# One core, a Mamba-2 block beside a gated feed-forward layer: the order of the first batch is rewritten, and one product moves to GpSimd

## The chip, the core and the metric

The kernel runs on one core of a Trainium2 chip. Its time is device time in microseconds (us). A core has four compute engines that run their own instruction streams side by side and meet through semaphores: TensorE (matrix products into the eight PSUM banks of 512 fp32 columns), VectorE, ScalarE and GpSimd; SyncE's queue and ScalarE's queue start the transfers. In the profile they are PE (and PEld for weight loads), DVE, ACT, POOL and SP.

## The reference

`x` has 4 sequences of 512 tokens with 512 channels. Everything is fp32.

```python
xn  = (x - mean(x)) / sqrt(var(x) + 1e-5)                  # over the 512 channels
out = x + (xn + mamba2(xn)) + ffn(xn)

def mamba2(u):                                             # 16 heads of 64, state 128
    z, xBC, dt = split(u @ w_in)                           # 1024, 1024 + 128 + 128, 16
    dt  = softplus(dt + dt_bias)
    xBC = silu(causal_conv4(xBC, conv_w) + conv_b)         # 4 taps along the tokens
    X, B, C = split(xBC)
    y = ssd(X * dt, dt * -exp(A_log), B, C) + X * D        # state-space scan
    y = y * silu(z)
    y = y * rsqrt(mean(y * y) + 1e-5) * norm_w
    return y @ w_out

def ffn(u):
    h = silu(u @ W1.T) * (u @ W3.T)                        # 2048 wide
    return fwht(h) @ W2.T                                  # Walsh-Hadamard over 2048
```

## The kernel before, in words

The four sequences ("batches") run one after the other. Each matrix product is made in three fp16 passes: the operands are split into a high and a low half (`hi`, `lo`), and hi*hi, hi*lo and lo*hi are summed in PSUM (`three`, L541). So that the halves fit fp16, each weight group is scaled by a power of two that comes from a bound on its sum of squares. This costs the first batch much preparation which the others don't have: it reads the fp32 weights, squares and sums them, scales and splits them, and writes the halves to `w_parts` in HBM, from which batches 1 to 3 load them.

The unit of work is a weight tile: 128 output channels by 512 tokens, 12 matmuls of 512 columns. Ten C tiles (x, B, C, with the convolution), eight Z tiles (the gate), sixteen pairs A, U (W1, W3), then sixteen G steps (W2). All engines walk one list per batch, `SCHEDULES[b]`, and each executes its own part of each token; that list alone sets the order on each engine. In batch 0 it begins with `FIRST`; behind it, tokens are placed by the count of A and U and G tiles before them (`FIRST_AT`, `STEP_AT`, `PREP_AT`). The tokens the change touches:

- `C`, `Z`, `A`, `U`: TensorE projects a tile (`project`); ScalarE and VectorE finish it (`finish`). For C, ScalarE starts an accumulator (L860), VectorE adds three taps (L1121), ScalarE makes a tanh (L875) and VectorE the silu (L1103), which frees one of two accumulators. In batch 0 ScalarE and VectorE first split the tile that is `AHEAD` = 3 places further on (L823, L1084).
- `G1S`: ScalarE squares the last two pieces of the second w_in group, TensorE sums them (L580), VectorE makes the second scale (`scale_g1`), which all tiles from the fifth on need for their split. The first scale, of four tiles and w_dt, is made before the loop.
- `KA`, `K`, `KS`: squares of W1 (ScalarE, L897) and W3 (GpSimd, L1294) from a ring of five buffers, their sums on TensorE (L636, L641), and the scale of W1 and W3.
- `DT`, `SUM`: projection of dt, softplus, cumulative sums. `WOL`, `WOQ`, `WOS`, `WOH`: load, squares, scale and split of w_out.
- `F`: half of the Hadamard transform of one W2 block: TensorE multiplies (L649), ScalarE squares the block for the W2 scale (L800) and copies the product (L908) into one of two buffers, SyncE stores it to `w2_mid` (L503). `H`: the other half (L661, L917, L1185). `W2S` makes the W2 scale that H needs.
- `T`, `X`, `S`, `R`, `Y`, `N`, `Q`, `V`, `W`: the scan, four chunks of 128 tokens per batch. `T` includes XD = X * D on ScalarE (L951) and Xdec on GpSimd (L1309); TensorE needs Xdec at `S`, VectorE XD at `Y`.
- `LN`, `XT`: normalisation of the next sequence (VectorE L998 to L1009, ScalarE L757) and its transposes (TensorE L555), copied out as `xh` (ScalarE L763) and `xl` (VectorE L1015).

A tile's PSUM bank is one of three in turn, so TensorE waits at a tile for the eviction of the tile, or F product, three places before (`make_banks`, `claim`). H has bank 4 alone.

## Time and profile before

| | us |
|---|---|
| median of 3 runs | 1010.45 (1009.56 to 1012.27) |
| the profiled execution | 1006.74 |
| its span | 1004.9 |

| engine | busy, us | share |
|---|---|---|
| PE | 941.8 | 94% |
| DVE | 597.8 | 59% |
| ACT | 391.2 | 39% |
| POOL | 264.3 | 26% |

The span runs from the first to the last instruction. A busy TensorE says only that matmuls were under way; a matmul at the lower of its two clocks (1.2 instead of 2.4 GHz) is busy twice as long. The granted clock is shown as a share of 2.4 GHz. An idle time is put down to the instruction that ended it, the releaser. Rows beginning with L541 are matmuls of any token, as all go through one helper. The share of busy time of an engine says little on a program of stages: the question is, stage by stage, which wait TensorE had.

### The profile page before, as it was taken

To read this page: it belongs to the slowest core of one execution; us is meant where nothing else is said; L and a number is where in the kernel's file an instruction comes from. 1 tells how busy PE (TensorE), PEld (TensorE's weight loads), DVE (VectorE), ACT (ScalarE), POOL (GpSimd) and SP (SyncE) were. 2 spreads that over 40 slices of the span, in tenths; PEclk is the share of its full clock that TensorE was granted. 3 is DMA by queue.
4 is the path that set the end of the run, shared out by engine and by line. 5 is a ranking of instruction groups with operands and counts; after the bars stand their busy time and mean duration, and the time that the engine had idled before them with its cause. 6 is when DMAs were issued, how large, how long until landed. Compare 5 with 4: busy or idle time off the path is not lost.

```text
span 1004.9 us, 13326 instructions
## 1 busy us (share of the span) xinstructions
PE 941.8 (94%) x4960; PEld 469.0 (47%) x4960; DVE 597.8 (59%) x1064; ACT 391.2 (39%) x680; POOL 264.3 (26%) x164
## 2 busy tenths in 40 slices
PE   3799779899989999999999999999999999999997
PEld 2334335444434445554544445555544445555543
DVE  5687477688633565757651666666651666666621
ACT  5576764635222334442321334442321344343200
POOL 0132343452000201645200201654400201645300
PEclk9899899999989999999999999999999999999999
DMA  9579454664422434554322434554322534355123
GB/s 330 202 263 389 154 180 142 236 199 148 157 76 82 162 96 112 168 149 118 121 65 63 170 95 115 158 157 126 105 66 61 174 95 135 92 157 147 44 74 95
DMA packets 80944, 142.65 MB, mean 142 GB/s; under 512 B 8176, under 2 KB 21104, under 8 KB 78832
## 3 DMA queue, kind: packets, MB, share of 16 engines
q1 hardware_dynamic: 61808, 113.83, 35.6%
q10 hardware_dynamic: 19072, 27.97, 9.3%
q8 instruction: 40, 0.66, 0.3%
q14 instruction: 24, 0.20, 0.1%
HBM read 115.82 MB, written 25.95 MB: 141 GB/s over the span
## 4 chain that ended last, share of the span: by engine, by line
PE 79%; DVE 7%; ACT 6%; issue 4%; DMA 2%; POOL 1%; SPq 0%; ACTq 0%; DVEq 0%; POOLq 0%
PE ps L541 51%; PE ps L741 16%; PE ps L706 3%; PE ps L698 2%; PE ps L692 2%; PE ps L661 1%; DVE arena L1121 1%; DMA arena<-cs_rows 1%; PE ps L678 1%; ACT arena L800 1%; DMA arena<-w_dt 1%; ACT arena L823 1%; ACT arena L956 1%; DVE arena L1142 1%; DVE wo_lo L1194 1%
## 5 line engine op out<-in xcount | busy, mean ns | idle before, releaser
L541 PE MATMUL ps<-xh,arena 128*128 128x512 f16 x1600 | 494.8, 382 | 10.9 <-DVE arena L1121 5.0
L541 PE MATMUL ps<-xl,arena 128*128 128x512 f16 x800 | 305.9, 382 | 0.0
L541 PEld LDWEIGHTS ps<-xh,arena 128*128 128x128 f16 x1600 | 159.6, 100 | 203.3 <-issue 19.4
L741 PE MATMUL ps<-arena 128*128 128x512 f16 x768 | 173.3, 382 | 0.0
L1286 POOL TENSOR_TENSOR arena<-arena 128x512 f16<-128x512 f32 x64 | 83.0, 1298 | 293.8 <-ACT arena L870 293.7
L1301 POOL TENSOR_TENSOR arena<-arena 128x2048 f32<-128x2048 f32 x16 | 58.9, 3681 | 294.5 <-DMA arena<-cs_rows 294.5
L1121 DVE SCALAR_TENSOR_TENSOR arena<-ps,cw,arena 128x511 f32<-128x511 f32 (+2 forms) x120 | 89.6, 749 | 55.8 <-ACT arena L860 53.8
L541 PEld LDWEIGHTS ps<-xl,arena 128*128 128x128 f16 x800 | 78.7, 98 | 89.7 <-issue 5.0
L741 PEld LDWEIGHTS ps<-arena 128*128 128x128 f16 x768 | 75.1, 99 | 93.5 <-issue 9.1
L870 ACT ACTIVATE arena<-arena 128x512 f16<-128x512 f32 x64 | 40.3, 630 | 168.0 <-DVE arena L1142 168.0
L541 PE MATMUL ps<-wo_hi,arena 128*128 128x512 f16 x256 | 78.7, 379 | 1.2 <-DVE arena L1249 1.2
L865 ACT ACTIVATE arena<-ps,f 128x512 f32<-128x512 f32 x64 | 43.4, 678 | 81.9 <-PE ps L541 81.5
L1137 DVE SCALAR_TENSOR_TENSOR arena<-arena,ps 128x512 f32<-128x512 f32 x64 | 43.8, 684 | 46.3 <-ACT arena L865 46.3
L1084 DVE SCALAR_TENSOR_TENSOR arena<-arena,scl 128x512 f16<-128x512 f32 x50 | 47.8, 959 | 28.0 <-ACT arena L823 27.7
L1142 DVE SCALAR_TENSOR_TENSOR arena<-ps,arena 128x512 f32<-128x512 f32 x64 | 44.2, 690 | 24.4 <-PE ps L541 23.1
L1207 DVE TENSOR_TENSOR arena<-arena 128x2048 f32<-128x2048 f32 x16 | 38.4, 2399 | 28.6 <-ACT arena L956 28.5
L541 PE MATMUL ps<-wo_lo,arena 128*128 128x512 f16 x128 | 48.5, 379 | 0.0
L1275 DVE SCALAR_TENSOR_TENSOR arena<-ps,f_w,arena 128x512 f32<-128x512 f32 x16 | 10.9, 746 | 61.5 <-PE ps L741 61.5
L860 ACT ACTIVATE arena<-ps,cb,cw 128x512 f32<-128x512 f32 x40 | 31.0, 775 | 36.4 <-PE ps L541 32.2
L541 PEld LDWEIGHTS ps<-wo_hi,arena 128*128 128x128 f16 x256 | 25.1, 98 | 33.5 <-DVE arena L1246 2.7
L951 ACT ACTIVATE arena<-arena,dcol 128x128 f32<-128x128 f32 x128 | 39.0, 392 | 0.0
L865 ACT ACTIVATE arena<-ps,f_half 128x512 f32<-128x512 f32 x32 | 22.0, 686 | 40.9 <-PE ps L541 40.5
(157 smaller groups left out, 1073.7 us busy)
## 6 DMA issues: line engine op xcount, KB each, us to landing
arena<-w_parts SPq DMA_DIRECT2D x198, 256.0 KB, 2.7
w_parts<-arena SPq DMA_DIRECT2D x66, 256.0 KB, 3.2
arena<-cs_rows ACTq DMA_DIRECT2D x16, 1024.0 KB, 6.0
arena<-w SPq DMA_DIRECT2D x48, 256.0 KB, 7.0
arena<-w SPq DMA_DIRECT2D x8, 1024.0 KB, 14.1
arena<-ecs_rows ACTq DMA_DIRECT2D x24, 256.0 KB, 6.9
w_mid<-arena SPq DMA_DIRECT2D x16, 256.0 KB, 2.6
arena<-x ACTq DMA_DIRECT2D x16, 256.0 KB, 4.0
```

Source lines behind the costliest of these rows:

```text
L541: ins = nc.tensor.matmul(out_ap, lhs(i, a), rhs(i, c), start=(i == 0 and s == 0), stop=(i == n - 1 and s == 2))
L741: ins = nc.tensor.matmul(bank(t), hw[a][:, i, t * P:(t + 1) * P], w2s[i % W2R][:, d, :], start=(i == 0 and s == 0), stop=(i == JF - 1 and ...
L865: nc.scalar.activation(slot, src, ACT.Tanh, scale=(f_half if kind == "Z" else f_13)[:, 0:1]).then_inc(tanh_ok.sem, 1)
L870: nc.scalar.activation(hid_hi[:, i, :], hs[i % 2], ACT.Copy).then_inc(hid_h.sem, 1)
L951: ins = nc.scalar.activation(XD[:, q * P:(q + 1) * P], XT[:, q, c * P:(c + 1) * P], ACT.Copy, scale=dcol[:, q:q + 1])
L1084: nc.vector.scalar_tensor_tensor(out=part_lo[p % PARTS], in0=raw_tile(p), scalar=scl[:, n:n + 1], in1=part_hi[p % PARTS], op0=ALU.mult, op ...
L1121: ins = nc.vector.scalar_tensor_tensor(out=a[:, s:L], in0=src[:, 0:L - s], scalar=cw[:, i, TAPS - 1 - s:TAPS - s], in1=a[:, s:L], op0=ALU. ...
L1137: nc.vector.scalar_tensor_tensor(out=hs[i % 2], in0=tb[tanh[key] % 2], scalar=1.0, in1=src, op0=ALU.add, op1=ALU.mult).then_inc(evac.sem, 1)
L1142: nc.vector.scalar_tensor_tensor(out=hs[i % 2], in0=src, scalar=HID / (2 * XS * XS), in1=hs[i % 2], op0=ALU.mult, op1=ALU.mult).then_inc(e ...
L1207: nc.vector.tensor_tensor(Eb, Eb, Gm.unsqueeze(1).to_broadcast([P, NH, P]), ALU.mult).then_inc(m_ok.sem, 1)
L1286: nc.gpsimd.tensor_tensor(hid_lo[:, i, :], hs[i % 2], hid_hi[:, i, :], ALU.subtract).then_inc(hid_l.sem, 1)
L1301: nc.gpsimd.tensor_tensor(Eb, csbc, cs_s[:, c * NH:(c + 1) * NH].unsqueeze(2).to_broadcast([P, NH, P]), ALU.subtract).then_inc(esub_ok.sem, 1)
```

## The change

The first batch gets an order of its own; the other batches keep theirs.

- Start: w_dt is loaded by ScalarE's queue, and the first two w_in pieces signal one by one. ScalarE normalises the last quarter of x. The split of tile 0 is placed between the first and the second pair of xh and xl, and the constants that the first scale gives come behind the splits.
- `G1S` becomes two tokens: `G1Q` (ScalarE's squares) after the first tile, `G1S` (sum and scale) after the third. Tile 3 is split at tile 0; tiles 4, 5 and 6 together at tile 3 (`SPLITS`).
- `DT` is after Z0, `SUM` after K0, `KA1` one tile after `KA0`; squares of W1 and W3 have two buffers each, so that a KA waits for the sum of two before. `WOL` waits for the last K sum. Part 0 is stored ahead of the ring loads.
- Four F products stand before A0 instead of two, and the others follow one per A, U pair; W2 is loaded and squared two blocks at a time, in ScalarE's first F buffer.
- XD is made by one GpSimd instruction in `T`, ahead of Xdec, in all batches.
- `LN` of the next batch is at tile 28 instead of 35 in batch 0. Several scan steps stand one or two tiles later.
- The transposes for batch 1 use banks 6, 7, 5, 6 and for batches 2 and 3 banks 4 to 7, instead of 6 and 7 in turn; they wait for the eviction of the last W.

```diff
-FIRST = ("B G1S C C0 DT C1 Z0 SUM C2 KA0 Z1 C3 K0 KA1 Z2 WOL C4 K1 KA2 Z3 C5 K2 KA3 Z4 C6 K3 KS Z5 C7 Z6 E0 Z7 F0 F1 "
-         "A0").split()
+FIRST = ("B G1Q C C0 G1S C1 Z0 DT C2 KA0 Z1 KA1 C3 Z2 K0 SUM KA2 C4 Z3 K1 KA3 C5 Z4 K2 C6 Z5 K3 KS WOL C7 E0 Z6 Z7 "
+         "F0 F1 F2 F3 A0").split()
+SPLITS = {0: (3,), 3: (4, 5, 6)}
...
+PREP_FIRST = {"LN": 28}
...
-    steps = [(at, 0, (kind, b + 1)) for kind, at in PREP_AT.items() if b + 1 < NB]
+    steps = [(at if b else PREP_FIRST.get(kind, at), 0, (kind, b + 1)) for kind, at in PREP_AT.items() if b + 1 < NB]
...
-              for c, at in enumerate(places) if at is not None]
+              for c, at in enumerate(places if b else STEP_FIRST.get(kind, places)) if at is not None]
...
+def splits_at(p):
+
+    if p < max(SPLITS):
+        return SPLITS.get(p, ())
+    return SPLITS.get(p, (p + AHEAD,) if p + AHEAD < NT else ())
...
         def load_w2_raw(sp, k):
 
-            sp.wait_ge(w_lo.sem, w_lo.at(0, G0 - 2 + JF // 2 + k))
-            for m in (2 * k, 2 * k + 1):
-                sp.dma_start(w2_raw[m], w2[m]).then_inc(d_w2r[k], 16)
+            sp.wait_ge(w_lo.sem, w_lo.at(0, k + 3 if k % 2 == 0 else k + 10))
+            sp.dma_start(w2_pair[k].rearrange("p (n d) -> p n d", n=2),
+                         w2[2 * k:2 * k + 2].rearrange("n p d -> p n d")).then_inc(d_w2r[k], 16)
...
             sp.dma_start(at(raw_at, 2 * TILE).rearrange("p (n c) -> p n c", n=2),
-                         w_in[0:2].rearrange("n p c -> p n c")).then_inc(d_g0, 16)
-            sp.dma_start(staged[:, 0:2, :], w_in[2:4].rearrange("n p c -> p n c")).then_inc(d_g0, 16)
-            sp.dma_start(wdt_raw.rearrange("p k h -> p (k h)"), w_dt).then_inc(d_g0, 16)
+                         w_in[0:2].rearrange("n p c -> p n c")).then_inc(d_g0[0], 16)
+            sp.dma_start(staged[:, 0:2, :], w_in[2:4].rearrange("n p c -> p n c")).then_inc(d_g0[1], 16)
             for k, (lo, hi) in enumerate(G1_PIECES):
                 sp.dma_start(staged[:, lo - 2:hi - 2, :], w_in[lo:hi].rearrange("n p c -> p n c")).then_inc(d_g1[k], 16)
+            store_parts(sp, 0)
             for n in range(NRING):
                 load_ring(sp, n)
-            store_parts(sp, 0)
...
-                        if b == 0 and 0 <= p + 1 - (G0 - 2 + JF // 2) < JF // 2:
-                            load_w2_raw(sp, p + 1 - (G0 - 2 + JF // 2))
+                        if b == 0 and 9 <= p < 9 + JF // 2:
+                            load_w2_raw(sp, p - 9)
...
                     elif kind == "WOL":
                         sp.wait_ge(pe_xt.sem, pe_xt.at(0, NC - 1))
+                        sp.wait_ge(k_sums, KC)
                         sp.dma_start(wo_raw, w_out.rearrange("(q p) d -> p q d", p=P)).then_inc(d_wo, 16)
...
         def xt_bank(nb, t):
 
-            return bank(6 + t % 2) if nb else bank(4 + t)
+            return bank((6, 7, 5, 6)[t] if nb == 1 else 4 + t)
...
         def pe_transposes(pe, nb, quarters=range(NC)):
             for t in quarters:
-                pe.wait_ge(xn_ok.sem, xn_ok.at(nb, t))
-                if t >= 2 and nb > 0:
-                    pe.wait_ge(xl_ok.sem, xl_ok.at(nb, t - 2))
+                if nb > 0:
+                    pe.wait_ge(xn_ok.sem, xn_ok.at(nb - 1, t))
+                elif t < NC - 1:
+                    pe.wait_ge(xn_dve, t + 1)
+                else:
+                    pe.wait_ge(xn_act, 1)
+                if nb == 1 and t == 3:
+                    pe.wait_ge(xl_ok.sem, xl_ok.at(nb, 0))
...
                     elif kind == "XT":
                         pe.wait_ge(diag_read.sem, diag_read.at(b, NC - 1))
+                        pe.wait_ge(mamba_evac.sem, mamba_evac.at(b, NC - 1))
                         pe_transposes(pe, i)
...
             act.dma_start(con[:], consts[:, 0:4 * P]).then_inc(d_con, 16)
+            act.dma_start(wdt_raw.rearrange("p k h -> p (k h)"), w_dt).then_inc(d_wdt, 16)
...
-            act.wait_ge(d_g0, 48)
-            square(sq_act[:, 0:2 * TILE], at(raw_at, 2 * TILE), SQ_G0, sq_g0)
+            act.wait_ge(d_g0[0], 16)
+            square(sq_act[0][:, 0:2 * TILE], at(raw_at, 2 * TILE), SQ_G0, sq_g0)
             act.wait_ge(sq_g0, 1)
-            square(sq_act[:, 0:2 * TILE], at(hid_at, 2 * TILE), SQ_G0 + 1, sq_g0)
+            act.wait_ge(d_g0[1], 16)
+            square(sq_act[0][:, 0:2 * TILE], at(hid_at, 2 * TILE), SQ_G0 + 1, sq_g0)
             act.wait_ge(sq_g0, 2)
-            square(sq_act[:, 0:KD * NH], wdt_raw.rearrange("p k h -> p (k h)"), SQ_G0 + 2, sq_g0)
-            act_xh(act, 0)
+            act.wait_ge(d_wdt, 16)
+            square(sq_act[0][:, 0:KD * NH], wdt_raw.rearrange("p k h -> p (k h)"), SQ_G0 + 2, sq_g0)
+            act.wait_ge(ln_ok.sem, ln_ok.at(0, 0))
+            nc.scalar.activation(xraw[:, NC - 1, :], xraw[:, NC - 1, :], ACT.Identity, bias=nmr[:, NC - 1:NC],
+                                 scale=rstd[:, NC - 1:NC]).then_inc(xn_act, 1)
...
-            for p in range(AHEAD):
+            act_xh(act, 0, (0, 1))
+            split_hi(0)
+            act_xh(act, 0, (2, 3))
+            for p in range(1, AHEAD):
                 split_hi(p)
...
-                        if b == 0 and POS[0][kind, i] + AHEAD < NT:
-                            split_hi(POS[0][kind, i] + AHEAD)
+                        if b == 0:
+                            for p in splits_at(POS[0][kind, i]):
+                                split_hi(p)
                         finish((kind, i))
-                    elif kind == "G1S":
...
                     elif kind == "KA":
                         n = RING_AT["1", i]
                         act.wait_ge(d_ring[n % NRING], 16 * (n // NRING + 1))
                         if i == 0:
                             act.wait_ge(sq_g1, len(G1_PIECES))
-                        else:
-                            act.wait_ge(k_sums, i)
-                        nc.scalar.activation(sq_act, ring[n % NRING], ACT.Square).then_inc(k_act, 1)
+                        elif i >= 2:
+                            act.wait_ge(k_sums, i - 1)
+                        nc.scalar.activation(sq_act[i % 2], ring[n % NRING], ACT.Square).then_inc(k_act, 1)
                     elif kind == "F":
-                        act.wait_ge(d_w2r[i // 2], 32)
-                        if i > 0:
-                            act.wait_ge(sq_w2, i)
-                        square(w2_junk, w2_raw[i], SQ_W2 + i, sq_w2)
-                        act.wait_ge(f_done, i + 1)
                         if i == 0:
                             act.wait_ge(xt_done.sem, xt_done.at(0, MC - 1))
                         elif i >= 2:
                             act.wait_ge(d_mid[i % 2], 16 * (i // 2))
+                        if i % 2 == 0:
+                            act.wait_ge(d_w2r[i // 2], 16)
+                            square(w2m[0].bitcast(BF16), w2_pair[i // 2], SQ_W2 + i // 2, sq_w2)
+                            act.wait_ge(sq_w2, i // 2 + 1)
+                        act.wait_ge(f_done, i + 1)
                         nc.scalar.activation(w2m[i % 2], tile_bank(0, (kind, i)), ACT.Copy).then_inc(f_out_ok, 1)
...
-                        act.wait_ge(diag_read.sem, diag_read.at(b, c - 1))
-                        for q in range(QE):
-                            ins = nc.scalar.activation(XD[:, q * P:(q + 1) * P], XT[:, q, c * P:(c + 1) * P], ACT.Copy,
-                                                       scale=dcol[:, q:q + 1])
-                        ins.then_inc(xd_ok.sem, 1)
...
-            for t in range(NC):
+            for t in range(NC - 1):
                 nc.vector.tensor_scalar(xraw[:, t, :], xraw[:, t, :], rstd[:, t:t + 1], nmr[:, t:t + 1], ALU.mult,
-                                        ALU.add).then_inc(xn_ok.sem, 1)
+                                        ALU.add).then_inc(xn_dve, 1)
...
             dve_xl(dve, 0, (0, 1))
+            split_lo(0)
+            dve_xl(dve, 0, (2, 3))
+            for p in range(1, AHEAD):
+                split_lo(p)
...
-            dve_xl(dve, 0, (2, 3))
...
-            for p in range(AHEAD):
-                split_lo(p)
...
-                        if i > 0:
-                            pool.wait_ge(k_sums, i)
+                        if i >= 2:
+                            pool.wait_ge(k_sums, i - 1)
                         for s in range(4):
...
                     elif kind == "T":
+                        pool.wait_ge(xt_done.sem, xt_done.at(b, MC - 1))
+                        pool.wait_ge(diag_read.sem, diag_read.at(b, c - 1))
+                        nc.gpsimd.tensor_tensor(XD.rearrange("p (q l) -> p q l", q=QE), XT[:, 0:QE, c * P:(c + 1) * P],
+                                                dcol[:].unsqueeze(2).to_broadcast([P, QE, P]), ALU.mult).then_inc(xd_ok.sem, 1)
```

ScalarE at the second scale, the stretch before: squares (L800), split (L823), accumulator of a C tile (L860), tanh (L875).

```order
L800 ACTIVATE arena,row_sq<-arena 128x2048 x2
L823 ACTIVATE arena<-arena,scl 128x512
L860 ACTIVATE arena<-ps,cb,cw 128x512
L800 ACTIVATE arena,row_sq<-arena 128x2048
L800 ACTIVATE arena,row_sq<-arena 128x1024
L823 ACTIVATE arena<-arena,scl 128x512
L860 ACTIVATE arena<-ps,cb,cw 128x512
L875 ACTIVATE arena<-arena 128x512
L823 ACTIVATE arena<-arena,scl 128x512
```

The same stretch of the change, where the squares are L820, splits L847, accumulators L889 and tanh L904.

```order
L820 ACTIVATE arena,row_sq<-arena 128x2048 x2
L847 ACTIVATE arena<-arena,scl 128x512
L889 ACTIVATE arena<-ps,cb,cw 128x512
L820 ACTIVATE arena,row_sq<-arena 128x2048
L820 ACTIVATE arena,row_sq<-arena 128x1024
L889 ACTIVATE arena<-ps,cb,cw 128x512
L904 ACTIVATE arena<-arena 128x512
L889 ACTIVATE arena<-ps,cb,cw 128x512
L904 ACTIVATE arena<-arena 128x512
L847 ACTIVATE arena<-arena,scl 128x512 x3
L889 ACTIVATE arena<-ps,cb,cw 128x512
L904 ACTIVATE arena<-arena 128x512
```

The two squares stay behind the first accumulator, but the fifth tile's split now stands behind those of three C tiles, and three splits stand together.

ScalarE at the F products, with waits, before: tanh of Z7 (L865), squares of W2 (L800), copies (L908).

```order
L823 ACTIVATE arena<-arena,scl 128x512 [waits tile_done,d_wst0,scale_13,d_raw2]
L865 ACTIVATE arena<-ps,f_half 128x512 [waits tile_done,evac]
L800 ACTIVATE arena,row_sq<-arena 128x512 [waits d_w2r0]
L908 ACTIVATE arena<-ps 128x512 [waits xt_done,f_done]
L800 ACTIVATE arena,row_sq<-arena 128x512 [waits sq_w2,d_w2r0]
L908 ACTIVATE arena<-ps 128x512 [waits f_done]
L823 ACTIVATE arena<-arena,scl 128x512 [waits tile_done,d_wst1,scale_13,d_raw3]
L865 ACTIVATE arena<-ps,f 128x512 [waits tile_done,xt_done]
L922 ACTIVATE arena,row_sq<-arena,nw 128x512 [waits d_wo]
L922 ACTIVATE arena,row_sq<-arena,nw 128x512 [waits sq_wo,d_wo]
```

And in the change: squares of two blocks (L820), copies (L938).

```order
L847 ACTIVATE arena<-arena,scl 128x512 [waits tile_done,d_wst0,scale_13,d_raw2]
L894 ACTIVATE arena<-ps,f_half 128x512 [waits tile_done,evac]
L820 ACTIVATE arena,row_sq<-arena 128x1024 [waits d_w2r0,xt_done]
L938 ACTIVATE arena<-ps 128x512 [waits f_done,sq_w2]
L938 ACTIVATE arena<-ps 128x512 [waits f_done]
L820 ACTIVATE arena,row_sq<-arena 128x1024 [waits d_w2r1,d_mid0]
L938 ACTIVATE arena<-ps 128x512 [waits f_done,sq_w2]
L938 ACTIVATE arena<-ps 128x512 [waits f_done,d_mid1]
L847 ACTIVATE arena<-arena,scl 128x512 [waits tile_done,d_wst1,scale_13,d_raw3]
L894 ACTIVATE arena<-ps,f 128x512 [waits tile_done,xt_done]
L952 ACTIVATE arena,row_sq<-arena,nw 128x512 [waits d_wo]
```

Four copies stand ahead of the first A, and the second square waits for the store of the first copy (`d_mid0`).

VectorE at the normalisation of the next sequence, before: `V` and `H` (L1185), then the statistics (L998).

```order
L1185 SCALAR_TENSOR_TENSOR arena<-ps,f_had,arena 128x512 x2
L1235 COPY arena<-ps 128x1
L1237 TENSOR_SCALAR arena<-arena 128x1
L1240 TENSOR_SCALAR arena<-arena 128x1
L1242 TENSOR_SCALAR arena<-arena 128x1
L1231 TENSOR_REDUCE arena<-arena 128x128
L1185 SCALAR_TENSOR_TENSOR arena<-ps,f_had,arena 128x512
L998 BN_STATS arena<-arena 128x6 x4
L1000 MEMSET arena 128x4
L1002 BN_AGGR arena<-arena 128x2 x4
L1004 TENSOR_SCALAR arena<-arena 128x4
```

And in the change (statistics L1023, split L1098, gates L1163 and L1168).

```order
L1098 SCALAR_TENSOR_TENSOR arena<-arena,scl 128x512
L1163 SCALAR_TENSOR_TENSOR arena<-arena,ps 128x512
L1239 TENSOR_TENSOR arena<-ps,arena 128x1024
L1098 SCALAR_TENSOR_TENSOR arena<-arena,scl 128x512
L1168 SCALAR_TENSOR_TENSOR arena<-ps,arena 128x512
L1023 BN_STATS arena<-arena 128x6 x4
L1025 MEMSET arena 128x4
L1027 BN_AGGR arena<-arena 128x2 x4
L1029 TENSOR_SCALAR arena<-arena 128x4
L1006 TENSOR_SCALAR arena<-arena 128x4
```

They stood between two H; now they stand behind U13, ahead of W of the third chunk.

## Rows read from the trace of the kernel before

**Rows 1.** Windows: busy us of each engine, TensorE's clock, DMA share, GB/s.

```profile
0.00:300.00 300.00, 251.81 (x1214) 122.01 (x1215) 198.58 (x371) 160.32 (x285) 81.50 (x56) 0.94 0.61 207
300.00:1005.00 705.00, 689.97 (x3749) 347.01 (x3746) 399.23 (x693) 230.90 (x395) 182.78 (x108) 1.00 0.39 114
20.00:87.00 67.00, 55.93 (x277) 24.88 (x278) 48.14 (x86) 42.96 (x59) 18.69 (x16) 0.90 0.74 274
```

**Rows 2.** Timeline of TensorE: start, us, line, operation, count, idle before and its releaser.

```profile
19.96 0.40 PE L541 MATMUL ps<-xh,arena 128*128 128x512 f16 x1 [3.02 <-DVE arena L1084]
...
28.50 0.56 PE L580 MATMUL ps<-row_sq,con 128*128 128x5 f32 x2 [4.09 <-ACT arena L800]
...
44.94 0.43 PE L570 MATMUL ps<-arena,con 128*128 128x64 f32 x2 [1.86 <-DVE arena L1040]
...
57.67 1.82 PE L636 MATMUL ps<-arena 128*128 128x512 bf16 x4 [2.46 <-ACT arena L897]
...
83.42 1.04 PE L641 MATMUL ps<-arena 128*128 128x512 bf16 x4 [2.28 <-POOL arena L1294]
...
120.03 2.08 PE L649 MATMUL ps<-arena,hads 128*128 128x512 f32 x2 [4.34 <-DVE arena L1142]
...
146.88 0.58 PE L720 MATMUL ps<-cmean,arena 128*128 128x1 f32 x2 [4.68 <-DVE arena L1231]
...
184.60 1.06 PE L678 MATMUL ps<-con,arena 128*128 128x128 f32 x8 [2.15 <-issue]
...
280.31 2.07 PE L661 MATMUL ps<-arena,hads 128*128 128x512 f32 x2 [5.26 <-DVE arena L1185]
```

**Rows 3.** Windows of TensorE alone: us, busy, clock, DMA share, GB/s.

```profile
120.00:125.00 5.00, 4.68 (x7) 0.50 0.40 114
```

**Rows 4.** Chain of waits: start, us, what.

```profile
29.06 5.05 PE ps L541 x12
...
154.37 2.59 PE ps L541 x12
```

**Rows 5.** Timeline of ScalarE.

```profile
11.79 1.06 ACT L800 ACTIVATE arena<-arena 128x1024 bf16<-128x1024 f32 x1 [5.74 <-DMA arena<-w_dt]
...
27.21 1.06 ACT L800 ACTIVATE arena<-arena 128x1024 bf16<-128x1024 f32 x1
...
112.15 2.43 ACT L951 ACTIVATE arena<-arena,dcol 128x128 f32<-128x128 f32 x8
```

**Rows 6.** Timeline of VectorE, first 20 us.

```profile
17.96 1.29 DVE L1015 SCALAR_TENSOR_TENSOR xl<-ps,xh 128x512 f16<-128x512 f32 x2
```

**Rows 7.** Groups by line in 0 to 300: busy us, mean ns, idle before.

```profile
L823 ACT ACTIVATE arena<-arena,scl 128x512 f16<-128x512 f32 x50 | 35.4, 712 | 3.3 <-DVEq L1163 1.9 <-DMA w_parts<-arena 0.8 <-ACT arena L784 0.5
...
L1121 DVE SCALAR_TENSOR_TENSOR arena<-ps,cw,arena 128x511 f32<-128x511 f32 (+2 forms) x30 | 22.5, 749 | 8.0 <-ACT arena L860 7.4
...
L860 ACT ACTIVATE arena<-ps,cb,cw 128x512 f32<-128x512 f32 x10 | 7.8, 775 | 10.0 <-PE ps L541 5.9 <-DVE arena L1103 4.0
...
L1103 DVE SCALAR_TENSOR_TENSOR arena<-arena 128x512 f32<-128x512 f32 x10 | 6.8, 683 | 0.0
```

**Rows 8.** The page's DMA issues: count, KB each, us to landing.

```profile
w_mid<-arena SPq DMA_DIRECT2D x16, 256.0 KB, 2.6
```

**Rows 9.** VectorE and GpSimd timelines, 175 to 185, and the line of Xdec.

```profile
180.27 2.49 DVE L1084 SCALAR_TENSOR_TENSOR arena<-arena,scl 128x512 f16<-128x512 f32 x1 [0.93 <-ACT arena L823]
...
178.05 4.17 POOL L1301 TENSOR_TENSOR arena<-arena 128x2048 f32<-128x2048 f32 x1 [4.60 <-DMA arena<-cs_rows]
...
L1309 POOL TENSOR_TENSOR arena<-arena x12: 1900/1906/2335, 111.4 to 894.6; 128x1024 f32<-128x1024 f32 x12
```

**Rows 10.** VectorE and ScalarE timelines around the next batch's normalisation.

```profile
270.29 2.46 DVE L998 BATCH_NORM_STATS2 arena<-arena 128x6 f32<-128x512 f32 x4
...
275.97 2.93 ACT L757 ACTIVATE arena<-arena 128x512 f32<-128x512 f32 x4 [6.38 <-DVE arena L1009]
```

**Rows 11.** Who waited for whom, whole span: us in total, times, longest.

```profile
PE ps L555 <- DVE xl L1015: 3.5, 3, 1.4
```

66 lines of the change are left out of this document (37 added, 29 removed).

## The prediction

> **What bounds the kernel now.** I read the windows first. TensorE is busy for 689.97 of the 705 us after 300, at a granted clock of 1.00, and for 251.81 of the first 300, at a mean of 0.94 [rows 1]. Batches 1 to 3 are bound by TensorE; only the first batch, which also prepares all weights, has time to win. Of its 48.2 idle us (300 less 251.81), 12.5 are the wait for the first normalised tile, which the change leaves. TensorE's timeline, read next for its idle times, gives the places of the rest [rows 2]: 3.02 before the first projection at 19.96; 4.09 at 28.50, where the sum for the second scale waits for ScalarE's squares; 1.86 at 44.94 (dt); 2.46 at 57.67 (first K); 2.28 at 83.42 (last K, GpSimd); 4.34 at 120.03; 4.68 at 146.88; 2.15 at 184.60; 5.26 at 280.31 (the sixth H). After the long ones the clock is at its lower level: 0.50 in 120 to 125, behind the 4.34 [rows 3]. A tile of 12 matmuls takes 5.05 us at 1.2 GHz and 2.59 at 2.4 [rows 4], so a gap costs its length and half of what then runs slowly.
>
> **The start.** ScalarE's squares waited 5.74 us for w_dt, until 11.79 [rows 5]. With w_dt on ScalarE's queue they start a microsecond or more earlier; but the sum stands behind the first transposes on TensorE, which are bound by x and its normalisation, so it comes only about 0.1 us sooner. More comes from VectorE's queue: before, the first split follows the last xl, at 19.25 (17.96 + 1.29 [rows 6]), and the constants stand between the xl pairs. Now split 0 is between the pairs and the constants are behind: the last xl, and with it TensorE's first projection, comes at about 19.0, 0.9 us earlier.
>
> **The second scale.** Before, TensorE waits for ScalarE's squares (the last one 27.21 + 1.06 [rows 5]) after one tile. Now it runs tiles 1 and 2 meanwhile. But VectorE makes the scale behind the evictions of three C tiles. I walk them with [rows 7]: squares done at 28.0, ScalarE's accumulator for tile 1 (0.78) 28.8, VectorE's three taps (3 x 0.75) 31.1, the silu of tile 0 (0.68), which frees the accumulator, 31.7, accumulator 32.5, taps 34.85, the scale's chain of small operations, some 1.1: 36.0. Then a split on ScalarE (0.71) and its low half on VectorE (about a tap's 0.75): the fifth tile, Z0, starts at 37.6, while TensorE ends C1 at 31.8. The 4.09 goes and a gap of 5.8 comes, later. Z0 began at 40.5 before (44.94 less 1.86 is its end, less 2.6), so it is now 2.9 ahead.
>
> From there the order is looser. K0 stands behind Z2 with its squares long done (2.46 gone, and 1.6 of slow clock on K0 and the tile behind); the sum over dt stands behind K0, which covers its 1.86; the ring is asked for earlier, w_out only after K3, and there are two buffers for squares, so GpSimd is ready for K3 (2.28 gone). My walk of the three queues gives new waits of 0.6 and 0.8 us for the taps of the tile three places before. Up to the end of K3 and Z5: before, 11.07 us idle (67 less 55.93 [rows 1]) and about 5.6 lost to the slow clock (half of 20 to 23, 29 to 34 and 58 to 61); now 7.2 idle and 3.6 (tile 0 and Z0 are still slow). With the start that is 0.9 + 3.9 + 2.0: **-7 us**; Z5 ends at 79.0.
>
> **The F block.** Each F product needs a bank, its copy by ScalarE and a store. Four now stand in a row, and the third waits for the first one's store, 2.6 us [rows 8]. By the walk C7, Z6 and Z7 end at 86.8; C7's taps, late behind the scale of W1 and W3 (82.9) and its split, end at 87.3, and its silu, for which the first square of W2 now waits, at 90.7. Square 1.25 and copies of 0.6: F0 92.6, F1 93.2; the store until 95.4, square and copies again: F2 97.3, F3 97.9. U0 takes F2's bank and starts at 97.4. TensorE has 10.6 us from 86.8 and work for 6.1 of them (four F at 0.87, one tile): 4.5 idle, before none. In return, two F products are done that stood later, and ScalarE saves a start and an accumulator read per pair.
>
> Up to 153, the 4.34 and 4.68 and the slow clock behind them give way to waits of 1 to 3 us at A3, T1, A5 and U5, for ScalarE arrives at A1's tanh only 0.5 us ahead of before. I get the end of U5 at 149.7 instead of 153.3, with two F more done (1.7): 5.4 ahead. So this stage gives back **+2 us** of the 7 (bounds 0 and +7, all of it). For 150 to 250 I take 0; the 2.15 at 184.60 may go.
>
> **D product on GpSimd.** ScalarE loses 2.43 us a chunk [rows 5]. GpSimd gets a 128 x 1024 product of two inputs; the nearest row, Xdec, takes 1.90 to 2.34 [rows 9]. Queued behind it are Xdec and the low half of the next U tile. TensorE asks for Xdec at S, three tiles (7.8 us) or more later in the chunks that have one, so this is covered; if that cover were gone it would cost the 2.3. In batches 1 to 3 ScalarE's saving is worth nothing, TensorE being the bound. I take 0, for the cover is three times the price. Bounds: -5 (two chunks of ScalarE's chain in 100 to 150) and +28 (twelve chunks of 2.34, all passed on to TensorE).
> VectorE's row speaks against this edit: the split that began at 180.27 took 2.49 us, and ended just after GpSimd's product of 178.05 + 4.17 [rows 9].
> The Trainium skill (SBUF — State Buffer, Who interferes with whom) says that a VectorE instruction with two SBUF inputs and a GpSimd instruction that reads SBUF exclude each other for a whole instruction. The trace agrees (2.49 us instead of 0.75). By this rule each D product may hold VectorE up once; what that would give is the rival "port".
>
> **The next normalisation at tile 28.** Before, it stands between two H on VectorE, from 270.29 to 275.97, and ScalarE's four xn (2.93) follow [rows 10], so that H6 waited 5.26 and, with a G tile, ran slowly: some 3.3 more. Now these 5.7 and 2.9 stand before W2 and A14, and TensorE has these two (5.2 and 2.6) for cover; but behind VectorE's part stand A14's split and gate, the scale of W2 and the eviction of U14, for which H0 and H1 wait. Walked from before's times, H0 starts at 250.1 instead of 246.8 and H1 at 255.5 instead of 251.8: 3.7 paid for 8.6. That is -4.9, and -2.4 if the new gap draws the clock down; -8.6 if the cover suffices. I take **-4 us**.
>
> **Transposes.** Three waits for xl, 3.5 us in all [rows 11], go with the extra banks; 0.5 stays at batch 1's last quarter: **-3 us**. The added wait for W3's eviction costs nothing, since two G steps (5.2 us) stand between.
>
> **Sum.** -7 + 2 + 0 - 4 - 3 = -12. The profiled execution of 1006.74 us (its span 1004.9 and 1.84 around it) would take 994.7. It lies 3.7 below the median of the runs shown, 1010.45, on which the forecast stands: **998.5 us**.
>
> **Rivals.**
> "All of it", 0.19: the F block costs nothing because ScalarE is ahead, 184.60 goes, the normalisation is covered: -7 + 0 - 2.2 - 8.6 - 3.5 = -21.3, 989. For it: ScalarE has room in every window. Against: in 100 to 150 ScalarE and VectorE release the banks.
> "Given back", 0.20: ScalarE's chain of squares, copies, scales and w_out from 95 to 150 sets the pace as before, and the normalisation costs at its new place nearly what it saves: -7 + 6 - 1 - 3 = -5, 1005.5. For it: A1's tanh only 0.5 ahead. Against: ScalarE loses two D products there.
> "Port", 0.05: the D products of batches 1 to 3 hold up VectorE's evictions. It decides where VectorE's reserve in a T step is under 2.34 us; if six of ten are passed on, 0.6 x 28 = +17 - 12 = +5, 1015.5. Against: VectorE is busy 399.23 of 705 us there [rows 1], and GpSimd's longer products leave TensorE at 98%.
> My sum has 0.56.
>
> **How the numbers follow.** Runs of this kernel lie within 0.3% (3 us), below which I call it no change. Faster by more: my sum, "all of it" and two thirds of "given back", 0.88; within it the rest and a mild "port", 0.08; slower 0.04. The range, 989 to 1007, holds my case, "given back" and the upper half of "all of it".
>
> **What would show it.** The first projection at 19.0; a gap of 5 to 6 us before Z0, none at K0 and K3; 4 to 5 us idle around F0 to F3; no 5 us between H5 and H6 but 3 before H0; no wait for L1015 in batches 2 and 3; batch 1 starting 11 us earlier, and the rest as long as before. I am wrong if batches 1 to 3 change by over 4 us, if Z0's gap is absent or twice as long, or if 87 to 153 gains time.

## The result, and the profile after

The changed kernel takes **1006.88 us** (median of 20 runs, 1001.30 to 1009.59) against 1010.75 of the kernel before in the same rounds: ratio 0.9964, 95% interval 0.9951 to 0.9976. That is 3.9 us less, where 12 less was forecast. The time lies in the range given, 8.4 us above the 998.5 forecast; the size of the gain does not fit. Of the rivals, "given back" (5 less) comes nearest in time.

The profiled execution took 1008.38 us, and lies above the median of its kernel; that of before (1006.74) lies below. So both were profiled once more (experiments 9 and 10). Markers on TensorE, in us: the first F, the 16 products of the second chunk's state (S1), those of the last chunk (S3), and the sum over dt for the second, third and fourth batch:

| execution | first F | S1 | S3 | 2nd | 3rd | 4th | span |
|---|---|---|---|---|---|---|---|
| before | 94.66 | 156.79 | 231.88 | 330.38 | 555.60 | 779.77 | 1004.9 |
| before again | 95.45 | 160.69 | 235.73 | 332.77 | 556.65 | 780.51 | 1005.5 |
| after | 88.94 | 161.32 | 237.84 | 333.77 | 557.92 | 781.34 | 1006.6 |
| after again | 89.04 | 160.39 | 236.99 | 332.69 | 555.25 | 777.78 | 1004.8 |

The lead of 6.1 us at the first F (means) is gone at S1. These traces put the two kernels level; both of before are faster than its median, so the 4 us of the timed difference stand in no trace, and I can't place them.

The first row of after answers to [rows 1], the others to [rows 3] (columns: stretch, its length, busy time of PE, PEld, DVE, ACT, POOL, granted clock, DMA share, GB/s).

```profile
300.00:1006.00 706.00, 693.38 (x3764) 349.40 (x3762) 417.14 (x694) 203.36 (x300) 208.55 (x120) 1.00 0.40 115
...
100.00:105.00 5.00, 1.72 (x5) 0.65 (x6) 0.73 (x2) 3.61 (x7) 0.00 (x0) 0.50 0.22 83
150.00:155.00 5.00, 2.60 (x7) 0.96 (x8) 4.93 (x8) 1.61 (x2) 1.10 (x1) 0.62 0.16 52
255.00:260.00 5.00, 2.06 (x3) 0.80 (x4) 4.02 (x10) 3.17 (x4) 0.00 (x0) 0.70 0.00 0
```

TensorE's timeline after, with the idle time ahead of each piece, against [rows 2]:

```profile
19.32 0.58 PE L554 MATMUL ps<-xh,arena 128*128 128x512 f16 x1 [2.27 <-DVE xl L1040]
38.80 0.61 PE L554 MATMUL ps<-xh,arena 128*128 128x512 f16 x1 [6.08 <-DVE arena L1098]
...
103.28 0.59 PE L554 MATMUL ps<-xh,arena 128*128 128x512 f16 x1 [5.50 <-ACT arena L938]
...
152.40 0.59 PE L554 MATMUL ps<-xh,arena 128*128 128x512 f16 x1 [5.93 <-DVE arena L1163]
170.51 0.38 PE L554 MATMUL ps<-xh,arena 128*128 128x512 f16 x1 [2.93 <-DVE arena L1168]
257.94 2.08 PE L679 MATMUL ps<-arena,hads 128*128 128x512 f32 x2 [5.00 <-DVE f_had L1204]
```

The gaps of before at the second scale, the first and the last K are gone, and the 5.8 forecast ahead of Z0 is there with 6.08. Behind it stand three that the forecast had smaller or not at all: 5.50 before U0, 5.93 before A5, 5.00 before the first H, each with the clock down behind it. What released U0, in the chain of waits of 92 to 106 (start, us, what), and SyncE's request for w_out ahead of it:

```profile
93.42 0.61 ACT arena L938
...
94.04 7.30 DMA w_mid<-arena
...
101.36 0.03 ACT arena L820
```

```profile
81.02 0.38 SPq L530 DMA_DIRECT2D arena<-w_out  x1
```

ScalarE copied F0 and F1, and SyncE issued the store of F0 at 94.04. The square of the next pair writes where that store reads, so ScalarE sat idle for 6.86 us until it had landed, 7.30 after its issue and not the 2.6 of [rows 8]. F2's copy followed, and U0 needs F2's bank. Before A5 it is VectorE that is late (VectorE first, GpSimd below):

```profile
139.03 3.08 DVE L1098 SCALAR_TENSOR_TENSOR arena<-arena,scl 128x512 f16<-128x512 f32 x1 [1.83 <-ACT arena L847]
144.50 3.48 DVE L1221 SCALAR_TENSOR_TENSOR wo_lo<-arena,nws,wo_hi 128x512 f16<-128x512 f32 x2 [1.79 <-ACT wo_hi L956]
149.24 2.41 DVE L1098 SCALAR_TENSOR_TENSOR arena<-arena,scl 128x512 f16<-128x512 f32 x1
...
137.95 3.61 POOL L1328 TENSOR_TENSOR arena<-arena 128x2048 f32<-128x2048 f32 x1 [7.88 <-DMA arena<-cs_rows]
145.09 2.34 POOL L1336 TENSOR_TENSOR arena<-arena,dcol 128x1024 f32<-128x1024 f32 x1
```

L1336 is the D product. The two low halves of w_out beside it took 3.48 us.

### The profile page after: what moved, and what is told of

Its sections match the earlier page's. It is cut to its first block, busy times and chain, and to the rows that moved or that the text cites. A ratio compares the mean times of both kernels' runs of the same rounds, so it can differ in the third digit from the quotient of the medians.

```text
span 1006.6 us, 13195 instructions
## 1 busy us (share of the span) xinstructions
PE 941.3 (94%) x4960; PEld 469.3 (47%) x4960; DVE 619.2 (62%) x1063; ACT 352.7 (35%) x537; POOL 296.1 (29%) x180
## 4 chain that ended last, share of the span: by engine, by line
PE 75%; DVE 11%; issue 4%; ACT 4%; DMA 3%; POOL 2%; ACTq 0%; SPq 0%; DVEq 0%; POOLq 0%
PE ps L554 48%; PE ps L759 16%; DVE arena L1147 2%; PE ps L724 2%; DVE arena L1098 2%; DMA arena<-cs_rows 2%; PE ps L716 2%; PE ps L710 1%; PE ps L679 1%; PE ps L696 1%; POOL arena L1340 1%; DVE arena L1168 1%; DVE arena L1129 1%; DMA w_mid<-arena 1%; ACT arena L820 1%
## 5 line engine op out<-in xcount | busy, mean ns | idle before, releaser
L554 PE MATMUL ps<-xh,arena 128*128 128x512 f16 x1600 | 500.7, 386 | 35.5 <-DVE arena L1163 8.8
L759 PE MATMUL ps<-arena 128*128 128x512 f16 x768 | 171.2, 379 | 0.0
L1098 DVE SCALAR_TENSOR_TENSOR arena<-arena,scl 128x512 f16<-128x512 f32 x50 | 53.3, 1070 | 37.9 <-ACT arena L847 37.8
L1163 DVE SCALAR_TENSOR_TENSOR arena<-arena,ps 128x512 f32<-128x512 f32 x64 | 43.8, 684 | 47.4 <-ACT arena L894 47.4
L894 ACT ACTIVATE arena<-ps,f 128x512 f32<-128x512 f32 x64 | 43.5, 679 | 76.6 <-PE ps L554 76.6
L1168 DVE SCALAR_TENSOR_TENSOR arena<-ps,arena 128x512 f32<-128x512 f32 x64 | 44.1, 690 | 23.2 <-PE ps L554 22.2
L1234 DVE TENSOR_TENSOR arena<-arena 128x2048 f32<-128x2048 f32 x16 | 42.1, 2631 | 21.4 <-ACT arena L981 21.4
L1302 DVE SCALAR_TENSOR_TENSOR arena<-ps,f_w,arena 128x512 f32<-128x512 f32 x16 | 10.9, 746 | 61.5 <-PE ps L759 61.5
L889 ACT ACTIVATE arena<-ps,cb,cw 128x512 f32<-128x512 f32 x40 | 30.9, 773 | 31.3 <-PE ps L554 26.8
L904 ACT ACTIVATE arena<-arena 128x512 f32<-128x512 f32 x40 | 25.2, 630 | 38.6 <-DVE arena L1147 23.5
L847 ACT ACTIVATE arena<-arena,scl 128x512 f16<-128x512 f32 x50 | 35.3, 712 | 6.0 <-DVEq L1190 3.6
```

The costliest lines, as they stand in the source:

```text
L554: ins = nc.tensor.matmul(out_ap, lhs(i, a), rhs(i, c), start=(i == 0 and s == 0), stop=(i == n - 1 and s == 2))
L759: ins = nc.tensor.matmul(bank(t), hw[a][:, i, t * P:(t + 1) * P], w2s[i % W2R][:, d, :], start=(i == 0 and s == 0), stop=(i == JF - 1 and ...
L847: nc.scalar.activation(part_hi[p % PARTS], raw_tile(p), ACT.Copy, scale=scl[:, n:n + 1]).then_inc(w_hi.sem, 1)
L894: nc.scalar.activation(slot, src, ACT.Tanh, scale=(f_half if kind == "Z" else f_13)[:, 0:1]).then_inc(tanh_ok.sem, 1)
L1098: nc.vector.scalar_tensor_tensor(out=part_lo[p % PARTS], in0=raw_tile(p), scalar=scl[:, n:n + 1], in1=part_hi[p % PARTS], op0=ALU.mult, op ...
L1163: nc.vector.scalar_tensor_tensor(out=hs[i % 2], in0=tb[tanh[key] % 2], scalar=1.0, in1=src, op0=ALU.add, op1=ALU.mult).then_inc(evac.sem, 1)
```

## The experiments

Ratios are to the kernel before, timed in the same rounds, with 95% intervals; five rounds each but for 9 and 10. 0.001 is 1 us. Experiments 1 to 4 are edits of the changed kernel.

**1. No F copy or square of the first four waits for a store; F2 and F3 go to the words of XD** (0.9912, 0.9891 to 0.9933: 5.2 below the changed kernel).

```
-        w2m = [at(acc_at + s * D, D) for s in range(2)]
+        w2m = [at(a, D) for a in (acc_at, acc_at + D, Xdt_at + 5 * E, Xdt_at + 5 * E + D)]
...
+                            square(yh_junk if i < 4 else w2m[0].bitcast(BF16), ...)
```

> The changed kernel, but F2 and F3 are copied into two buffers of their own (words of the D product, which waits for their stores before it writes there), and the squares of the first two pairs of W2 go to a third place. So no copy and no square of the first four F waits for a store. Theory A (the wait for the store of F0 is what gave the front's gain back): ScalarE goes on right after F1's copy, the idle 5.50 us before U0 at 103.28 and the slow clock behind it go, U0 starts at 97 to 98, and the kernel is 3 to 6 us faster than the changed one (ratio to the kernel before 0.991 to 0.994). Rival B (a chain of ScalarE, VectorE and GpSimd between 110 and 160 sets the pace whatever the front does): the idle time goes at 98 and comes back as waits before A3, U4 and A5; within 1 us of the changed kernel (ratio 0.9955 to 0.9975).

```profile
112.07 0.38 PE L559 MATMUL ps<-xh,arena 128*128 128x512 f16 x1 [1.52 <-DVE arena L1175]
...
144.66 0.58 PE L559 MATMUL ps<-xh,arena 128*128 128x512 f16 x1 [5.94 <-DVE arena L1170]
```

The 5.50 is gone (U0 waits for nothing); A5 comes 7.7 us earlier (144.66, not 152.40), S1 at 153.30. Theory A holds, and the wait before A5 moved along unchanged, so it is another matter.

**2. w_out asked for behind F3's store** (0.9970, 0.9950 to 0.9991: no gain).

```
-  ... K3 KS WOL C7 E0 Z6 Z7 F0 F1 F2 F3 A0
+  ... K3 KS C7 E0 Z6 Z7 F0 F1 F2 F3 WOL A0
```

> The changed kernel, but w_out (2 MB) is asked for after F3's store instead of before C7, and the squares of w_out stand one tile later. If the store of F0 took 6.9 us instead of the 2.6 forecast because w_out, the reads of W1 and W3 and the stores of the parts shared the DMA engines at 85 to 100: it lands in 3 to 4 us, U0 starts at 99 to 100 instead of 103.3, and the kernel is 2 to 3 us faster than the changed one, unless ScalarE's squares of w_out then wait for their data at 104. Rival (the store waits for something else, or the gain is given back later): U0 stays at 103 or the time stays within 1 us of the changed kernel.

ScalarE and TensorE in this run:

```profile
95.94 1.06 ACT L820 ACTIVATE arena<-arena 128x1024 bf16<-128x1024 f32 x1 [1.57 <-DMA w_mid<-arena]
109.22 0.72 ACT L952 ACTIVATE arena<-arena,nw 128x512 bf16<-128x512 f32 x1 [4.16 <-DMA arena<-w_out]
...
113.08 0.38 PE L554 MATMUL ps<-xh,arena 128*128 128x512 f16 x1 [3.04 <-DVE arena L1163]
124.70 0.36 PE L598 MATMUL ps<-row_sq,con 128*128 128x9 f32 x2 [3.74 <-ACT arena L952]
```

The store of F0 now takes 2.01 us, and U0 waits for nothing. So w_out's 2 MB, with what queues behind them, are what made it slow. But ScalarE then waits 4.16 for w_out, and two gaps (3.04, 3.74) take the place of the 5.50. The cause was right, the expected gain of 2 to 3 us was not: the load is only moved.

**3. D product back on ScalarE** (0.9936, 0.9916 to 0.9956: 2.8 below the changed kernel).

```
+                        for q in range(QE):
+                            ins = nc.scalar.activation(XD[:, q * P:(q + 1) * P], XT[:, q, c * P:(c + 1) * P], ACT.Copy,
+                                                       scale=dcol[:, q:q + 1])
...
-                        nc.gpsimd.tensor_tensor(XD..., XT[:, 0:QE, ...], dcol..., ALU.mult)
```

> The changed kernel, but the D product is back on ScalarE, eight activations a chunk as before. The forecast had put the move at 0 (ScalarE's 2.43 us a chunk against cover on GpSimd). Theory A (GpSimd's 2.34 us product holds VectorE's low halves up at 139 to 151): the splits at 139 to 150 take 1 us and less again, the wait of 5.93 before A5 at 152.4 shrinks to about 3, and the kernel is 1 to 3 us faster than the changed one. Rival C (ScalarE is the one that sets the pace of 110 to 160, as before the change): the waits for its tanh grow and the kernel is 1 to 4 us slower than the changed one. Batches 1 to 3 within 1 us in either.

VectorE and TensorE at the same place:

```profile
140.19 2.19 DVE L1103 SCALAR_TENSOR_TENSOR arena<-arena,scl 128x512 f16<-128x512 f32 x1 [1.83 <-ACT arena L847]
144.77 1.85 DVE L1226 SCALAR_TENSOR_TENSOR wo_lo<-arena,nws,wo_hi 128x512 f16<-128x512 f32 x2 [1.79 <-ACT wo_hi L956]
148.49 1.79 DVE L1103 SCALAR_TENSOR_TENSOR arena<-arena,scl 128x512 f16<-128x512 f32 x1 [0.54 <-ACT arena L847]
...
151.03 0.38 PE L554 MATMUL ps<-xh,arena 128*128 128x512 f16 x1 [4.29 <-DVE arena L1168]
```

The pair of low halves takes 1.85 instead of 3.48: it takes 1.84 or 1.85 in every trace that has the product on ScalarE and leaves the pair together, and 3.48 or 3.49 in each that has it on GpSimd in batch 0. A5 waits 4.29 instead of 5.93, but that alone shows nothing: in the second execution of the changed kernel, with the pair at 3.48, it waits 4.24, for TensorE ran the tiles before at a lower clock (0.82 in 140 to 150) and came later.

```profile
151.82 0.59 PE L554 MATMUL ps<-xh,arena 128*128 128x512 f16 x1 [4.24 <-DVE arena L1163]
```

The splits stay near 2 us, for GpSimd's other products stand beside them: the expected 1 us and the 3 before A5 were too hopeful. Batches 1 to 3 did change, against both expectations (experiment 7).

**4. The next normalisation back at tile 35** (0.9987, 0.9967 to 1.0007: 2.3 above the changed kernel).

```
-PREP_FIRST = {"LN": 28}
+PREP_FIRST = {}
```

> The changed kernel, but the next normalisation of batch 0 is back at tile 35. The forecast had put the move at -4, so that this is 4 us slower than the changed kernel (ratio 1.000). The trace of the changed kernel speaks for less: 5.00 us idle and a slow clock before H0 instead of 5.26 before H6, so 0 to 1.5 us slower (ratio 0.9965 to 0.998).

2.3 lies between the two expectations, and the intervals allow either.

**5. Free buffers and D product on ScalarE** (0.9867, 0.9842 to 0.9893). **11. The same kernel again** (0.9877, 0.9855 to 0.9899); its edit of the front's order was without effect, since the table of the changed kernel was set again further down.

> The changed kernel with both undone costs together: F2 and F3 in buffers of their own (as in the first experiment) and the D product on ScalarE (as in the third). The first gave -5.2 and the third -2.8 against the changed kernel (ratios 0.9912 and 0.9936 against 0.9964). If the two act at different places, their sum: ratio 0.988 (0.987 to 0.9895), 998 us or less. If the product on ScalarE takes back in 100 to 150 what the free buffers gave (ScalarE has the F copies there as well), 0.990 to 0.992.

> The kernel of the fifth run (free buffers, D product on ScalarE, ratio 0.9867), with the order of the front (up to Z7) as before the change: the second scale ahead of the second tile, one K behind each square, three tiles of splits ahead; the second buffers for squares stay. The forecast had put the front at -7. If that was right and nothing behind it takes it back: 6 to 8 us slower than the fifth run (ratio 0.993 to 0.995). If the front's gain is absorbed later also there: within 2 us of the fifth run.

This is the fastest version: 12 to 13 us under the kernel before, 9 under the changed one, a little more than the sum of 5.2 and 2.8. Its gaps:

```profile
113.91 0.38 PE L559 MATMUL ps<-xh,arena 128*128 128x512 f16 x1 [2.55 <-DVE arena L1182]
...
144.92 0.59 PE L559 MATMUL ps<-xh,arena 128*128 128x512 f16 x1 [4.35 <-DVE arena L1177]
163.03 0.38 PE L559 MATMUL ps<-xh,arena 128*128 128x512 f16 x1 [2.84 <-DVE arena L1182]
246.01 1.81 PE L684 MATMUL ps<-arena,hads 128*128 128x512 f32 x2 [3.85 <-DVE f_had L1218]
```

Up to A5 the product on ScalarE wins nothing here: A5 starts at 144.92 (144.84 in 11) and at 144.66 in experiment 1, for ScalarE's eight activations make the wait at 113.91 2.55 us instead of 1.52. What it does win is at the first H, 3.85 instead of 5.00. There a small operation of VectorE ends with the D product; the changed kernel first, then this one:

```profile
239.87 1.29 DVE L1012 TENSOR_TENSOR arena<-arena 128x1 f32<-128x1 f32 x1
238.27 2.88 POOL L1336 TENSOR_TENSOR arena<-arena,dcol 128x1024 f32<-128x1024 f32 x1
...
229.07 0.16 DVE L1026 TENSOR_TENSOR arena<-arena 128x1 f32<-128x1 f32 x1
```

All six traces with the normalisation at 28 and the product on GpSimd in batch 0 have 5.00 at the first H, and all six with it on ScalarE 3.85 to 3.88.

Experiments 6, 12, 13, 14 and 16 are one edit each of this kernel, to be read against 0.987.

**6. The halves of w_out one a tile, tiles 7 to 13** (0.9904, 0.9879 to 0.9930: 3 slower).

> As the run before it, but the halves of w_out are made one a tile, at tiles 7 to 13, instead of two each at tiles 7 and 8. In the trace with the free buffers VectorE takes 3.49 us for the two low halves at 136.76, ahead of the chunk's product with dt, the split and the gate for which A5 waits 5.94. If this place is what holds A5 up: 1.5 to 3 us less than the run before it (ratio 0.985 to 0.9865). If A5 waits for GpSimd's hold on VectorE whatever stands in the queue: the same as the run before it within 1 us. If the eighth half now makes the first product with w_out wait at tile 14: up to 2 us slower.

```profile
144.81 0.38 PE L559 MATMUL ps<-xh,arena 128*128 128x512 f16 x1 [3.70 <-DVE arena L1177]
...
172.25 0.39 PE L559 MATMUL ps<-wo_hi,arena 128*128 128x512 f16 x1 [2.13 <-DVE wo_lo L1235]
```

A5 gains 0.65 only, and the product with w_out waits 2.13 for the eighth half: the third case of the expectation, which allowed 2.

**7. D product on ScalarE in batches 1 to 3 only** (0.9955, 0.9938 to 0.9973).

> The changed kernel, with the D product on ScalarE in batches 1 to 3 only (in batch 0 it stays on GpSimd). With it on ScalarE throughout, batches 1 to 3 took 670.4 us in the trace and 672.8 with it on GpSimd, and the first batch was 3.2 shorter. If the move costs TensorE time in the later batches, as the rival called port has it: ratio 0.9935 to 0.9945, 2 to 2.5 us below the changed kernel. If the gain sits in batch 0 (the split at 139 to 151): within 0.7 us of the changed kernel (0.9957 to 0.9971).

The timing can't tell it from the changed kernel. The traces can: from the second batch's sum over dt to the fourth's, the ten executions with the product on ScalarE take 445.0 to 445.7 us (445.31 here); the six with it on GpSimd 445.1 to 448.1, mean 447.0; before, with the old transposes, 449.39 and 447.74. So it costs 1.6 us in batches 1 and 2. To the end of the program, batch 3 included, the means are 670.5 and 672.7: 2.2 us. The rest of its price, 0.6 to 1.8 of the 2.8 and 4.0 timed, lies in batch 0.

What costs them is that S waits for Xdec, at the third chunk of a batch. The six traces with the product on GpSimd have one or two such waits, 1.0 to 2.8 us in all; the ten with it on ScalarE, and both of before, have none. In the changed kernel (GpSimd, VectorE, TensorE):

```profile
451.52 1.90 POOL L1336 TENSOR_TENSOR arena<-arena,dcol 128x1024 f32<-128x1024 f32 x1
453.37 3.96 POOL L1340 TENSOR_TENSOR arena<-arena 128x1024 f32<-128x1024 f32 x1
...
452.41 3.15 DVE L1234 TENSOR_TENSOR arena<-arena 128x2048 f32<-128x2048 f32 x1 [2.58 <-ACT arena L981]
...
457.38 1.98 PE L716 MATMUL ps<-arena 128*128 128x512 f32 x4 [1.18 <-POOL arena L1340]
```

The same place before, Xdec and the product that needs it:

```profile
449.10 1.91 POOL L1309 TENSOR_TENSOR arena<-arena 128x1024 f32<-128x1024 f32 x1
...
452.42 1.88 PE L698 MATMUL ps<-arena 128*128 128x512 f32 x4
```

There Xdec ended 1.41 us ahead. The D product puts 1.90 in front of it, and then Xdec itself, beside VectorE's product, takes 3.96. Where no such wait falls into the stretch to the fourth batch's sum, as in the second execution of the changed kernel, it takes 445.1, as with ScalarE.

**8. A0 between F1 and F2** (0.9959, 0.9938 to 0.9981).

> The changed kernel, with nothing but the order altered: A0 stands before F2 and F3 instead of behind them. If the 5.5 us before U0 is the store of F0 (6.9 us to land) and not the order: F2's copy is as late as before, U0's bank is now another one's, and A0's tanh runs in the wait, so that only 0.5 to 2 us are won (ratio 0.9945 to 0.996). If four F in a row are the fault themselves: most of the 5 us that the free buffers gave (0.992 to 0.9935).

```profile
97.10 0.38 PE L554 MATMUL ps<-xh,arena 128*128 128x512 f16 x1 [1.69 <-DVE arena L1163]
101.59 1.12 PE L667 MATMUL ps<-arena,hads 128*128 128x512 f32 x2 [1.74 <-ACT arena L938]
```

The gap is split, not closed, and the time is the changed kernel's, as the first case had it: it is the store, not the four F in a row.

**9, 10. Both kernels profiled again**: the table above.

> The kernel before, profiled once more. Its first profiled execution (1006.74 us) lies at the fast end of its runs (1006.92 to 1012.91) and the one of the changed kernel (1008.38) at the slow end of its own, so that their traces differ by +1.6 where the medians differ by -3.9. Another execution should show how much of the stages before 320 moves by itself: I expect the sum over dt of the second batch at 330 to 335 (330.38 in the first), with the difference in the F stores and the clock behind them, and batches 1 to 3 within 1 us of 674.5.

> The changed kernel, profiled once more. I expect the wait for F0's store again (4 to 6 us idle before U0), the 5.9 before A5 and the 5.0 before the first H; the second batch's sum over dt at 329 to 334 (333.77 in the first), and batches 1 to 3 within 1 us of 672.8.

As expected, but for batches 1 to 3 of the second execution of before (672.7, not 674.5) and the wait before A5 in that of after (4.24, not 5.9).

**12. Scale of W2 ahead of the normalisation, at 28 and 29** (0.9938, 0.9917 to 0.9960: 7 slower). **14. Normalisation at tile 26** (0.9907, 0.9886 to 0.9927). **16. At tile 35** (0.9908, 0.9890 to 0.9926).

> The kernel of the fifth run, with the scale of W2 ahead of the next normalisation on VectorE (scale at tile 28, normalisation at 29). There the first H waits 3.85 us for the scale, which stands behind the normalisation. If that order is what holds H0 up: the wait goes, ScalarE's four normalised tiles and VectorE's work then hold H1 up by 1 to 2 us instead, and the run is 1 to 3 us faster than the fifth (ratio 0.984 to 0.986). If the same work merely waits one H later: within 1 us (0.986 to 0.988).

> The kernel of the fifth run with the next normalisation at tile 26 instead of 28. At 28 the first H waits 3.85 us for the scale behind it, at 29 with the scale ahead of it 10.79 us were idle at the H. If the chain from VectorE's statistics over A14 to the scale is what the H waits for: at 26 VectorE has 5 us more, the wait before H0 falls under 1 us and 2 to 3 us are won (ratio 0.984 to 0.9855). If the chain then holds up T3 and S3 instead, at 217 to 229: no gain or up to 2 us lost (0.987 to 0.989).

> The fifth run's kernel with the next normalisation at tile 35, as before the change. In the fourth run this cost 2.3 us against the changed kernel. With ScalarE and VectorE relieved, the first H waits 3.85 us instead of 5.00 at tile 28, while the 5.25 before the sixth H at tile 35 stays: 2 to 4 us slower than the fifth and eleventh runs (ratio 0.989 to 0.991). If the place of the normalisation is worth nothing there: 0.986 to 0.988.

TensorE in 12, 14 and 16:

```profile
257.10 2.07 PE L684 MATMUL ps<-arena,hads 128*128 128x512 f32 x2 [10.79 <-DVE arena L1226]
```

```profile
236.85 3.36 PE L715 MATMUL ps<-arena 128*128 128x128 f32 x14 [7.79 <-ACT arena L985]
```

```profile
277.52 2.07 PE L684 MATMUL ps<-arena,hads 128*128 128x512 f32 x2 [5.25 <-DVE arena L1226]
```

The first two missed both of their expectations: 12 was to be faster or the same, 14 faster or up to 2 slower. 16 came as expected. At 29 an H waits 10.79 for the eviction of the one before it, which stands behind the normalisation on VectorE and ScalarE; at 26 the last chunk's state waits 7.79 for ScalarE's copy, behind the normalised tiles. Tile 28 is a good place: 3.6 us better than 35.

**13. The front in the order of before, second buffers kept** (0.9906, 0.9886 to 0.9925). **15. One buffer each for squares as well** (0.9911, 0.9893 to 0.9929).

```
-FIRST = ("B G1Q C C0 G1S C1 Z0 DT C2 KA0 Z1 KA1 C3 Z2 K0 SUM KA2 C4 Z3 K1 KA3 C5 Z4 K2 C6 Z5 K3 KS WOL C7 E0 Z6 Z7 "
+FIRST = ("B G1Q G1S C C0 DT C1 Z0 SUM C2 KA0 Z1 C3 K0 KA1 Z2 C4 K1 KA2 Z3 C5 K2 KA3 Z4 C6 K3 KS WOL Z5 C7 Z6 E0 Z7 "
```

> The kernel of the fifth run with the order of the front as before the change (in the eleventh run this edit had no effect, since the old table stood behind it in the file; that run repeats the fifth: 0.9877 and 0.9867). The second buffers for squares stay. The new order brings TensorE to the first F 6.1 us earlier (88.99 against 95.05, means of two executions each). If that lead comes through: 5 to 7 us slower than the fifth and eleventh runs (ratio 0.992 to 0.9945). If ScalarE and VectorE between 95 and 235 absorb it: within 2 us (0.986 to 0.989). If the lead comes from the second buffers and not from the order, the first F stands at 89 to 91 and the time within 2 us as well.

> The thirteenth run's kernel (front in the order of before) with one buffer each for ScalarE's and GpSimd's squares, as before the change. In the thirteenth the first F stood at 90.14, against 89.2 with the new order and 95.05 before. If the second buffers give the front its gain: the K wait for squares again (2.5 at the first, 2.3 at the last), the first F stands at 93 to 95, and the time is 3 to 5 us above the thirteenth run (ratio 0.9935 to 0.9955). If w_out's later load and the earlier start give it: the first F at 90 to 91 and within 1.5 us of the thirteenth (0.989 to 0.992).

TensorE in 13:

```profile
28.05 0.56 PE L603 MATMUL ps<-row_sq,con 128*128 128x5 f32 x2 [4.39 <-ACT arena L825]
44.89 0.43 PE L593 MATMUL ps<-arena,con 128*128 128x64 f32 x2 [2.70 <-DVE arena L1079]
57.27 1.03 PE L659 MATMUL ps<-arena 128*128 128x512 bf16 x4 [1.01 <-ACT arena L932]
```

The order is worth 3.4 us at the end (0.9906 against 0.9872, the mean of 5 and 11; the intervals allow 1 to 6), between the two expectations. 1.4 of it show at the first F (90.14 here, 89.2 and 88.3 there) and 2.2 at S1 (155.50 against 153.94 and 152.70). 4.39 + 2.70 + 1.01 make 8.1 us idle, and the new order has its 6 to 7 before Z0 and 1.2 and 0.8. With single buffers the first F stands at 92.27, but the time is the same within its interval. The first K waits 2.46 for squares again, but no K waits for GpSimd: it was not the second buffer that took the 2.28 at the last K away. That w_out's later load did is likely, and not tested alone.

## Why the prediction was wrong, point by point

| step | forecast | measured |
|---|---|---|
| front | -7 | -6.1 at the first F |
| F block, to S1 | +2 | +6.4 in the traces; free buffers give back 5.2, timed |
| 150 to 250 | 0 | +3.2, S1 to S3 |
| D product on GpSimd | 0 | +2.8; +4.0 with free buffers (experiment 1 against 5 and 11) |
| normalisation at 28 | -4 | -2.3; -3.6 in the relieved kernel |
| transposes | -3 | -3.2 in batches 1 and 2 |

(F block: 71.9 us from the first F to S1 instead of 63.7, less 1.74 for two F more. S1 to S3: 76.5 instead of 75.1, and two F less. A part of the D product's price is in these rows too. The sum of the traces' stages is near 0, as their spans are; it is not that of the timed runs.)

**The start and the second scale** were right: first projection at 19.32 (19.0 forecast), a gap of 6.08 (5.8), none at K0 and K3. But what I took for the order's doing is partly that of the second buffers and of what else changed there: with the old order the first F comes 1.4 us later, not 4, with single buffers for squares another 2.1, and 2.8 remain to the 95.05 of before.

**The F block** is the first step that failed, and the largest. "The third waits for the first one's store, 2.6 us [rows 8]" took the median of 16 stores. This one was issued at 94.04, when the DMA engines were full (share 1.02 in 90 to 95), and took 7.30. The same change had moved w_out's 2 MB from 59.62 to 81.02. They had landed by then (81.02 + 10.9 = 91.9), but the loads and stores asked for behind them had not: each took 11 to 13 us, and the last, asked for at 89.56, landed at 100.7. In the 15 traces with w_out asked for 13 to 15 us ahead of it the store took 5.4 to 7.4, in experiment 2 2.0. In the five with the changed kernel's copies and order, U0 waited 3.0 to 5.5; 5.50 is the upper end. The bound of +7 held, the value of +2 did not. ScalarE, which I held for the pace-setter of this stage, is busy for 35.03 of the 66 us from 87 to 153, before for 46.24: it had room, and waited.

**150 to 250**, taken at 0, failed as well, and neither the store nor the D product explains it: from S1 to S3 experiment 1 takes 76.6 us and experiment 3 76.7, like the changed kernel. Most of it is the wait of 2.93 at 170.51 (U6), with the clock at 0.67 in 170 to 175, where before had neither. U6 waits for VectorE's gate of U5 (L1168). Before, V0's operations stood ahead of A5's gate and X1's product behind it (first three rows: gate, product, gate); the change moved V0 to the tile of X1, and both now stand between A5's gate and U5's (last two), V0's between 165.32 and 169:

```profile
158.80 0.68 DVE L1137 SCALAR_TENSOR_TENSOR arena<-arena,ps 128x512 f32<-128x512 f32 x1
159.40 2.28 DVE L1207 TENSOR_TENSOR arena<-arena 128x2048 f32<-128x2048 f32 x1
...
162.26 0.68 DVE L1142 SCALAR_TENSOR_TENSOR arena<-ps,arena 128x512 f32<-128x512 f32 x1
...
163.11 2.29 DVE L1234 TENSOR_TENSOR arena<-arena 128x2048 f32<-128x2048 f32 x1 [0.92 <-ACT arena L981]
...
169.68 0.69 DVE L1168 SCALAR_TENSOR_TENSOR arena<-ps,arena 128x512 f32<-128x512 f32 x1
```

This is read from the traces; no experiment moved V0 back, so its worth is not shown.

**The D product** is the third step that failed. "Three tiles (7.8 us) or more" counted the cover from T; but Xdec stands behind all else on GpSimd's queue and before the change ended 1.41 us ahead of S in the second batch's third chunk. So the cover was gone there, and S waits for Xdec for 1.0 to 2.8 us in batches 1 to 3 (experiment 7). That is what the forecast priced at 2.3 a chunk "if that cover were gone". The rival "port", that VectorE's evictions are held up there, is not what the traces show as the wait, though GpSimd and VectorE do lengthen each other's work: it costs 2.2 us in batches 1 to 3, not 17. In batch 0 no S waits for Xdec; the price comes through VectorE, whose operations with two inputs take longer beside the product, and 1.15 us of it show before the first H. [Rows 9] showed that, and I wrote it down. The Trainium skill (SBUF — State Buffer, Who interferes with whom) has a VectorE instruction with two SBUF inputs and a GpSimd instruction that reads SBUF keep each other out. The traces agree: 3.48 us for two low halves beside the product, 1.85 without it. How often such an operation in batch 0 then holds TensorE up was not to be had from one row: with free buffers A5 comes no earlier without the product, while the wait before the first H shrinks by 1.15 us, as much as the small operation there.

**The normalisation**: 5.00 us idle before the first H instead of the 3.3 walked. With the D product on ScalarE it is 3.85, and the gain 3.6: so the -4 was right in size, but for what the D product added.

**The transposes** were right as far as the traces tell: 445.4 instead of 448.6 us for batches 1 and 2, where the two executions of before differ by 1.7. The D product took half of it back.

Experiments 5 and 11, without the store's wait and the product on GpSimd, measure what was forecast for the change, -12 (-13.4 and -12.4). That is luck in part: in them the F block is 0.9 better than before instead of 2 worse, and S1 to S3 2.0 worse instead of level. "Batch 1 starting 11 us earlier" failed; that batches 1 to 3 change by no more than 4 us held, and none of the signs of being wrong that I had named came.

What stays open: 4 us of the timed difference in no trace, what V0 beside X1 costs, and which of 0.7 us at the start, w_out's later load and the paired loads of W2 brings the first F from 95.05 to 92.27.

## What to carry to other kernels

Price a transfer by what else is in flight at its hour, not by the median of its kind, above all when the same change moves a large load next to it; and if a small store stands between two uses of a buffer, look for dead words elsewhere before reordering. Take the cover of a moved operation from the trace, as the time from the end of the last thing in its queue to the one that waits, and not from the place in the order. Work given to GpSimd can be paid by VectorE too: look in the trace for VectorE's operations that take longer beside it. A stage that gains in front is worth what the next stage lets through: name the first resource that is used earlier than before.

## What the runs showed of the hardware

The same 256 KB store took 2.0 us to land in experiment 2, with the DMA share at 0.52 in 90 to 95, and 7.3 in the changed kernel, with 1.02. The w_out load of 2 MB itself took 10.9 us to land (median 2.7 for 256 KB).

```profile
arena<-w_parts SPq DMA_DIRECT2D x198, 256.0 KB, 2.7
arena<-w_out SPq DMA_DIRECT2D x1, 2048.0 KB, 10.9
```

The same kernel differs by 4 us between two executions (spans 991.2 and 995.3), in part in the stretches behind gaps: in 5 the wait before U6 was 2.84 us and the clock in 150 to 200 0.99, in 11 it was 4.00 and 0.97.
